# Last attention group, its projection and the last rows by halves of the queries, in a two-layer gated cross-attention and MoE kernel

## The reference, cut to what matters

```python
x = x + tanh(g_xattn[1]) * xattn(layernorm(x), ctx)     # 16 heads of 16
#   out = softmax(q k^T * scale) v
#   h = relu(out @ W1 + b1);  return h @ W2 + b2         # 256 -> 512 -> 256
x = x + tanh(g_ffn[1]) * moe(layernorm(x))
#   logits = xn @ Wg + bg                                # 8 experts, top 2
#   h = relu(xn @ W1[e] + b1[e]); eo = h @ W2[e] + b2[e]; mixed by softmax of the top 2; layernorm
# layernorm(x) = (x - mean) / sqrt(var + 1e-5)
```

## Time and profile before

| | |
|---|---|
| median of 3 runs | 1501.73 us (1501.42 to 1502.45) |
| profiled execution, its own time | 1500.18 us |
| span of its records | 1498.4 us |
| TensorE busy, mean granted clock | 1351.1 us (90%), 0.951 |
| TensorE weight loads busy | 716.5 us (48%) |
| ScalarE busy | 975.1 us (65%) |
| VectorE busy | 549.3 us (37%) |

### The profile page before, as it was taken

How to read it: one execution, slowest core, us unless ns; L and a number is a source line. 1 busy time by engine, 2 the same in 40 slices (tenths; PEclk the granted TensorE clock), 3 DMA queues, 4 the chain that set the end, 5 groups by cost and what they waited for, 6 DMA issues and landing times. The chain is left out here.

```text
span 1498.4 us, 31951 instructions
## 1 busy us (share of the span) xinstructions
PE 1351.1 (90%) x13236; PEld 716.5 (48%) x13236; DVE 549.3 (37%) x1242; ACT 975.1 (65%) x1162; POOL 175.6 (12%) x188
## 2 busy tenths in 40 slices
PE   7799999999999996999657999999999994399994
PEld 4433333333333654999533334334334333299983
DVE  7412152242423253443550222422422524544435
ACT  4499999999996323333137996995996990055532
POOL 2000000000001321333200000000000000166530
PEclk9899999999999997999878999999999997599997
DMA  7661010101011714111439110110111115012214
GB/s 209 157 119 27 20 26 20 27 20 26 23 33 60 247 56 142 40 47 47 109 93 179 26 27 15 34 27 16 33 27 46 65 33 166 18 58 75 72 59 166
DMA packets 65866, 100.82 MB, mean 67 GB/s; under 512 B 10074, under 2 KB 47966, under 8 KB 64952
## 3 DMA queue, kind: packets, MB, share of 16 engines
q1 hardware_dynamic: 59768, 82.47, 20.2%
q0 software_dynamic: 5952, 16.26, 3.3%
HBM read 67.99 MB, written 26.21 MB: 63 GB/s over the span
## 5 line engine op out<-in xcount | busy, mean ns | idle before, releaser
L1182 ACT ACTIVATE arena<-ps 128x1024 f32<-128x1024 f32 x556 | 553.9, 1219 | 57.2 <-PE ps L948 57.2
L948 PE MATMUL ps<-arena 99*32 99x512 bf16 x6656 | 465.9, 384 | 15.4 <-PEq L798 9.4
L948 PEld LDWEIGHTS ps<-arena 99*32 99x32 bf16 x6656 | 151.3, 95 | 405.8 <-issue 167.0
L1182 ACT ACTIVATE wqkv<-ps 128x1024 f32<-128x1024 f32 x276 | 294.3, 1221 | 22.7 <-PE ps L948 22.7
L964 PE MATMUL ps<-arena 128*32 128x512 f32 x2224 | 290.5, 594 | 1.0 <-ACT arena L1182 0.8
L1264 DVE COPY work<-ps 128x512 f32<-128x512 f32 x32 | 22.1, 692 | 405.4 <-PE ps L964 405.4
L1652 PEld LDWEIGHTS ps<-work,arena 128*128 128x128 f32 x1184 | 144.6, 195 | 6.5 <-DVE work L1745 3.5
L1652 PE MATMUL ps<-work,arena 128*128 128x128 f32 x1184 | 145.7, 279 | 2.1 <-DVE work L1745 2.1
L964 PE MATMUL ps<-wqkv,arena 128*32 128x512 f32 x1104 | 144.0, 593 | 0.0
L1842 POOL DMA_INDIRECT work<-xn_img,fetch x62 | 60.9, 983 | 628.7 <-POOLq L928 612.8
L1664 PE MATMUL ps<-arena,work 128*128 x496 | 117.2, 380 | 0.0
(11 more groups left out here) (204 smaller groups left out, 1157.7 us busy)
## 6 DMA issues: line engine op xcount, KB each, us to landing
arena<-in_ew SPq DMA_DIRECT2D x16, 512.0 KB, 5.3
arena<-q_img SPq DMA_DIRECT2D x32, 192.0 KB
arena<-y_tok SPq DMA_DIRECT2D x12, 512.0 KB, 6.3
arena<-k_img SPq DMA_DIRECT2D x8, 624.0 KB, 12.9
q_img<-work SPq DMA_DIRECT2D x18, 256.0 KB, 2.6
k_img<-work SPq DMA_DIRECT2D x21, 208.0 KB, 2.5
arena<-q_img SPq DMA_DIRECT2D x32, 128.0 KB
work<-work SPq DMA_DIRECT2D x128, 32.0 KB, 2.0
```

The costliest lines, as they stand in the source:

```text
L948: last = nc.tensor.matmul(ps[i * VW:(i + 1) * VW, buf + j, :], k2[0:ROWS + SHIFT, h, at:at + VW], q2[0:ROWS + SHIFT, h, :], start=True, st ...
L1182: nc.scalar.activation(probs[(b * STEPS + u) % RING], ps[:, buf:buf + 2, :], ACT.Exp, scale=SCALE).then_inc(s_exp, 1)
```

## The change

It has four parts.

1. The last group (both layers). VectorE's new `last_group` drops the copy of the bank, spreads the sums as before, and then inverts and multiplies the first 256 queries and after them the second 256, reading the bank itself. SyncE's new `gather_last` moves each half with 4 DMAs of its own (8 in all, each of half the size) as soon as it is multiplied; the second half has a semaphore of its own, `s_oh2`. In layer 0, TensorE's first pair of projection tiles waits also until both halves are multiplied, the second pair for the second half's DMAs.
2. Layer 1's `last_projection` makes all hidden blocks of the first half (16 matmuls of 256 columns instead of 8 of 512), then of the second, then the output of the first two tiles, then of the last two. VectorE's new `own_tail` follows in halves.
3. The bias b2 of the last rows is added to x ahead of time (gate times b2), so x is updated straight from the banks. Each pair of tiles takes its statistics at once.
4. The router's rows: xn gets only the mean taken off before the rows are turned; Newton's steps and the scaling of xn by the inverse root come after that, once the rows are turned (`s_rt`), and the logits are scaled by the inverse root as the router's bias is added (4 instructions of 8 columns instead of 1 of 32). SyncE stores the last rows after the scaling.

```diff
+        def norm_means(n):
             for t in range(n):
                 last = nc.vector.bn_aggr(mv[:, t, :], stats[:, t, :])
+            return last
+        def norm_root(step, n):
+            step(norm_means(n))
+            norm_newton(step, n)
...
                         t = 2 * pair + half
+                        if b == NB - 1 and half == 0:
+                            pe.wait_ge(s_on, NB * NG + 1)
+                        if b == NB - 1 and t == 2:
+                            pe.wait_ge(s_oh2, 16 * HG)
...
                     def last_projection():
-                        for i in range(2):
-                            pe.wait_ge(s_oc[i], NB * 16 * HG * NG // 2)
-                        pe.wait_ge(s_u, NB * NG)
-                        for f in range(4):
-                            for k in range(KD):
-                                last = nc.tensor.matmul(ps[:, f, :], w1[:, k, f * P:(f + 1) * P], oT[:, k, :],
-                                                        start=(k == 0), stop=(k == KD - 1))
+                        for half in range(2):
+                            cols = slice(half * 2 * P, (half + 1) * 2 * P)
+                            if half:
+                                pe.wait_ge(s_oh2, 16 * HG)
+                            else:
+                                for i in range(2):
+                                    pe.wait_ge(s_oc[i], NB * 16 * HG * NG // 2)
+                                pe.wait_ge(s_on, NB * NG)
+                            for f in range(4):
+                                if half:
+                                    pe.wait_ge(s_read7, use(NB, f))
+                                for k in range(KD):
+                                    last = nc.tensor.matmul(ps[:, f, cols], w1[:, k, f * P:(f + 1) * P], oT[:, k, cols],
+                                                            start=(k == 0), stop=(k == KD - 1), skip_group_check=True)
+                                last.then_inc(s_full7, 1)
+                        for half in range(2):
+                            if half:
+                                pe.wait_ge(s_on, NB * NG + 1)
+                            for f in range(4):
+                                pe.wait_ge(s_read7, use(NB, 4 * half + f))
+                                for t in range(2 * half, 2 * half + 2):
+                                    last = nc.tensor.matmul(ps[:, 4 + t, 0:D],
+                                                            hidT[:, f, t * P:(t + 1) * P], w2[:, f, :],
+                                                            start=(f == 0), stop=(f == 3))
                             last.then_inc(s_full7, 1)
...
+                    def last_group():
+                        g, n = NG - 1, NB * NG
+                        dve.wait_ge(s_pv, NB * NG * NC)
+                        nc.vector.stream_shuffle(out=sums, in_=ps[:, 6 + g % 2, :], mask=[DH] * VW).then_inc(s_copy, 1)
+                        dve.wait_ge(s_copy, n)
+                        for i in range(2):
+                            cols = slice(i * 2 * P, (i + 1) * 2 * P)
+                            nc.vector.reciprocal(sums[:, cols], sums[:, cols]).then_inc(s_inv, 1)
+                            if i == 0:
+                                dve.wait_ge(s_oc[g % 2], (NB * NG // 2 - 1) * 16 * HG)
+                            dve.wait_ge(s_inv, n + i)
+                            nc.vector.tensor_tensor(o_norm[:, g % 2, cols], ps[:, 6 + g % 2, cols], sums[:, cols],
+                                                    ALU.mult).then_inc(s_on, 1)
+                        dve.drain()
...
+                    def own_tail():
+                        last_group()
+                        for half in range(2):
+                            cols = slice(half * 2 * P, (half + 1) * 2 * P)
+                            for f in range(4):
+                                dve.wait_ge(s_full7, use(NB, 4 * half + f))
+                                nc.vector.tensor_scalar(hidT[:, f, cols], ps[:, f, cols], b1[:, f:f + 1], 0.0,
+                                                        ALU.add, ALU.max).then_inc(s_read7, 1)
+                        for pair in range(2):
+                            dve.wait_ge(s_full7, use(NB, 8 + pair))
+                            rows = x[:, (NB - 1) * TB + 2 * pair:(NB - 1) * TB + 2 * pair + 2, :]
+                            nc.vector.scalar_tensor_tensor(out=rows, in0=ps[:, 4 + 2 * pair:6 + 2 * pair, 0:D], scalar=tg,
+                                                           in1=rows, op0=ALU.mult, op1=ALU.add).then_inc(s_xup[pair], 1)
+                            dve.wait_ge(s_xup[pair], NB)
+                            for i in range(2 * pair, 2 * pair + 2):
+                                nc.vector.bn_stats(stats[:, i, :], x[:, (NB - 1) * TB + i, :])
+                        dve.drain()
+                        step(norm_means(TB))
+                        for i in range(TB):
+                            last = nc.vector.tensor_scalar(xn[:, (NB - 1) * TB + i, :], x[:, (NB - 1) * TB + i, :],
+                                                           mv[:, i, 0:1], None, ALU.subtract)
+                        last.then_inc(s_ends, 1)
+                        norm_newton(step, TB)
+                        dve.wait_ge(s_rt, 1)
+                        for i in range(TB):
+                            last = nc.vector.tensor_scalar(xn[:, (NB - 1) * TB + i, :], xn[:, (NB - 1) * TB + i, :],
+                                                           rstd[:, i:i + 1], None, ALU.mult)
+                        last.then_inc(s_xs, 1)
...
+                        elif b == NB - 1:
+                            for t in range(TB):
+                                last = nc.vector.scalar_tensor_tensor(out=lg[:, b * TB + t, :], in0=got_logits[:, t, :],
+                                                                      scalar=rstd[:, t:t + 1], in1=rb[:, :],
+                                                                      op0=ALU.mult, op1=ALU.add)
...
-                    tail(NB, NB - 1)
+                    if l == 1:
+                        for pair in range(2):
+                            rows = x[:, (NB - 1) * TB + 2 * pair:(NB - 1) * TB + 2 * pair + 2, :]
+                            nc.vector.scalar_tensor_tensor(out=rows, in0=b2[:, :, :], scalar=tg, in1=rows, op0=ALU.mult,
+                                                           op1=ALU.add)
+                        dve.drain()
+                        own_tail()
+                    else:
+                        tail(NB, NB - 1)
                     route(NB - 1)
...
+                    def gather_last():
+                        g = NG - 1
+                        for i in range(2):
+                            cols = slice(i * 2 * P, (i + 1) * 2 * P)
+                            sp.wait_ge(s_on, NB * NG + i)
+                            for j in range(HG):
+                                h = HG * g + j
+                                sp.dma_start(oT[(h % 8) * DH:(h % 8 + 1) * DH, h // 8, cols],
+                                             o_norm[j * VW:j * VW + DH, g % 2, cols]
+                                             ).then_inc(s_oh2 if i else s_oc[g % 2], 16)
...
-                        sp.wait_ge(s_ends, NB)
+                        sp.wait_ge(s_xs, 1)
                         store_rows(NB - 1)
```

More of the change, by code:

```diff
@@ L433, in consts_pool, with norm_newton @@
                            allow_small_or_imprecise_dtypes=True)
-        def norm_root(step, n):
+        def norm_means(n):
             for t in range(n):
                 last = nc.vector.bn_aggr(mv[:, t, :], stats[:, t, :])
-            step(last)
+            return last
+        def norm_root(step, n):
+            step(norm_means(n))
+            norm_newton(step, n)
+        def norm_newton(step, n):
             step(nc.vector.tensor_scalar(var_e[:, 0:n], mv[:, 0:n, 1], EPS, None, ALU.add))
@@ L889, in layer @@
             s_xup = [sem(f"x_updated{l}_{i}") for i in range(2)]
+            s_oh2 = sem(f"oT_last_half_in{l}")
             s_ln = sem(f"moe_params_in{l}")
@@ L1277, in tail @@
                     def tail(b, now, first_group=None):
-                        group(now, NG - 1)
+                        if b == NB:
+                            last_group()
+                        else:
+                            group(now, NG - 1)
                         k = 0
-                        own = L.mlp and b == NB
                         if L.mlp:
@@ L1284, in tail @@
                                 dve.wait_ge(s_full7, use(b, k))
-                                nc.vector.tensor_scalar(hidT[:, f, :], ps[:, f if own else 7, :], b1[:, f:f + 1], 0.0,
+                                nc.vector.tensor_scalar(hidT[:, f, :], ps[:, 7, :], b1[:, f:f + 1], 0.0,
                                                         ALU.add, ALU.max).then_inc(s_read7, 1)
@@ L1290, in tail @@
```

(3 more changed lines are left out.)

## The result

| | before | changed |
|---|---|---|
| median, first comparison (6 runs each) | 1502.09 us (1501.33 to 1506.28) | 1491.20 us (1489.51 to 1495.98) |
| profiled execution, its own time | 1500.18 us | 1492.88 us |
| span | 1498.4 us | 1491.1 us |
| mean granted clock | 0.951 | 0.955 |

A forecast was written before the change was run, and what follows sets the result against it. From the attention's end in layer 1 to the logits, one engine works at a time. Savings of 7.4 + 0.45 - 0.45 + 0.25 = 7.65 us from 1501.73 gave 1494.1 us, range 1491.6 to 1497.0.

The forecast's parts named there:

- first half at TensorE: Layer 1's last group: copy dropped and first half sent early, so TensorE starts the projection at 1242.87, 2.49 us earlier.
- projection to output: Layer 1's hidden layer, from its start to the output's start: 7.07 us of matmuls plus 2.0 lost to low clock.
- output's end to turning: Layer 1's update and means: 3.5 us instead of 8.55, with the first pair covered and Newton's steps moved behind.
- turning to logits' step: Router's turning, copies and logits: 6.71 us before, less half of 0.93 for turning, with logits at the low clock.
- the logits' step: VectorE's scaling of the logits, 4 instructions of 8 columns instead of one: 0.45 us more.
- layer 0: Layer 0's projection: copy gone and halves there earlier, gaining between 0 and 0.89 us, taken as 0.25.
- The median of the runs is 1.55 above it: Base of the forecast: the median lies 1.55 us above the profiled 1500.18, so the sum is taken from 1501.73.
- about 1 us either way by the clock: Spread given to the forecast itself, from when TensorE's clock rises; each microsecond later costs 0.5.
- the clock high through the logits: Rival: TensorE's clock stays high through turning and logits until VectorE's scaling binds; 9.6 us gain, 1492.1 us; chance 0.14.
- The first half coming no earlier: Rival: TensorE in effect waits for all 8 DMAs, starting about 1245.3; 5.2 us gain, 1496.5 us; chance 0.15.
- the slower case: Rival: the clock does not rise in layer 1's projection; 5.0 us slower, 1506.7 us; chance 0.03.
- nothing: Rival: something else releases the experts' block, so the time stays at 1501 us; chance 0.04.

The follow-up runs named there:

- e11: Kernel before with extra unused matmuls in all TensorE waits from the attention's end to the experts' first tile in layer 1: 1494.06 us, ratio 0.9955.
- e12: Changed kernel with extra unused matmuls in all TensorE waits from layer 1's attention to the experts' first tile, same program as e8: 1487.17 us, ratio 0.9908.
- e3: Changed kernel with the halves undone in layer 1 only, 512 columns at once; other parts stay: 1495.34 us, ratio 0.9966.
- e5: Kernel before with extra unused matmuls in TensorE's waits: 10 ahead of the projection, 8 ahead of turning, 1 ahead of the logits: 1498.13 us, ratio 0.9982.
- e7: Changed kernel with each half's 4 DMAs in layer 1 issued by SyncE and ScalarE, two each: 1493.02 us, ratio 0.9946.
- e2: Changed kernel with part 4 alone undone, so xn is normalized whole before the rows are turned: 1496.72 us, ratio 0.9976.
- e8: Changed kernel with extra unused matmuls in all TensorE waits from the attention's end to the experts' first tile in layer 1: 1487.29 us, ratio 0.9917.
- e10: The changed kernel measured again without any edit: 1489.37 us, ratio 0.9922.
- e4: Changed kernel with extra unused matmuls in TensorE's waits: 7 ahead of the projection, 3 ahead of turning, 1 ahead of the logits: 1488.41 us, ratio 0.9922.
- e9: Changed kernel with extra unused matmuls in all those TensorE waits (as e8, but 6 ahead of the projection) and two DMA queues as in e7: 1486.67 us, ratio 0.9909.

## Why the prediction was wrong

**Each step against its measure** (changed kernel's first profile):

| term | predicted | measured |
|---|---|---|
| first half at TensorE | 2.49 earlier | 2.68 by the start, 0.07 of it from before the group: 2.61 |
| projection to output | 9.07 | 8.79 (clock's rise after 3.7, not 4.0) |
| output's end to turning | 3.5 | 3.31 (the subtractions took 1.14, not 1.38) |
| turning to logits' step | 6.30 | 5.88 (turning wholly at the high clock) |
| the logits' step | +0.45 | +0.44 |
| layer 0 | 0.25 | 0.25 at its place (10.40 us instead of 10.65 from the shared expert's start to the projection, load idle 0.24 instead of 0.89), 0.07 left at the last group |

The path came out 8.45 us shorter against my 7.65 less 0.25, 7.4. Mechanism, order and places held: no gap between the halves, the root hidden, VectorE free before the logits were. The rule of the Trainium skill (VectorE: DVE Perf Modes, Rules for kernel authors) against a larger count of VectorE operations, cited in the prediction, cost nothing here: the two inversions take 1.75 and 1.74 us where the one took 3.35, and what that is more lies behind what TensorE waits for. No run undoes the dropped copy, the early b2 or layer 0's part alone; what they are worth is read from rows.

**The step that failed** is "The median of the runs is 1.55 above it", and with it "about 1 us either way by the clock". I took a difference between one execution and the median of three for a constant, and forecast from 1501.73. Over five sets of runs the kernel before has a median of 1500.2 with single executions from 1496.8 to 1506.3; the changed kernel's profiled execution was 1.7 above its median, not 1.55 below it. These 3.2 us cover the whole miss of 2.9, for the profiled execution itself came as forecast (span 1490.8 forecast, 1491.1 measured). That was luck in part: its path was 1.05 us shorter than my sum, and its rest, in which I had put no difference, 1.2 us longer. Nor is the base the only thing off. In the first comparison the kernel before stood at 1502.09, and the gain was 10.9 instead of 7.65. Over all runs the forecast is 3.6 us above the changed kernel's 1490.5: 1.5 by the base and 2.1 by the gain. From 1500.2 the sum of 7.65 gives 1492.6, still 1.4 above the 1491.20 measured.

**What the sum did not hold.** The gain is 9.7 us over all runs, and the path gives 6.8 to 8.45. With extra matmuls in all waits the medians' difference is 6.9, near the path's 6.7 (e11, e12). So some 2.8 us of the gain are not there where the clock is mostly held; from the runs' spread I estimate an error of 1.5 us on this. It points to TensorE's clock, outside my terms, but it is not shown: the extra work occupies TensorE too, and no plain changed kernel stands beside that pair. That the levels of one kernel go with the clock is on record: of the changed kernel's 17 runs the ten with a mean granted clock of 0.956 or 0.957 took 1488.1 to 1490.9 us, the two with 0.952 took 1494.5 and 1496.0. What was seen of it in the profiles: turning at the high clock in one of three profiles (0.9), the rise in the projection between 3.7 and 5.2 us after its start (0.8), the rise at the start of the experts' loop after 7 or after 13.5 us, and the clock's fall ahead of the last sums. With these the rest moves between 194.0 and 200.8 in kernels that do not differ there.

The two places in the rest can be told apart. Where the rise at the loop's start comes late (e3, e5, e7), the sixth fetch is 17.8 to 18.0 us behind the first, and 14.8 to 16.1 in the others. From the last fetch to the end 55.6 to 56.6 us pass where the clock does not fall ahead of the last sums (e2, e3, e8, e10, e11), 57.9 to 59.3 where it does, and 60.1 to 60.2 in e5 and e7, where it stays low longer. A third spread lies ahead of the path: the last group begins between 1233.8 and 1237.7, and layer 0's 0.25 us cannot be seen in that. Whether the shorter waits of the change make the good cases more frequent there, or whether chance fell so in three sessions, stays open; 14 profiles do not settle it.

My rivals: the clock high through the logits was not seen in the changed kernel, and e4 shows its price: 58.00 - 54.58 = 3.4 us, of which 1.8 are the projection's (8.79 less 6.98) and the other 1.6 are near the 1.95 that I gave it. The first half coming no earlier is refuted by the start at 1242.68 and by e3, the slower case by the rise at 1246.36, "nothing" by the fetch.

## What to carry to other kernels

A chain with one engine at work at a time is added up well from single rows, and halving pays where the first half's way is the only one waited for. Before a sum is set against a median, ask how wide single executions lie; where they differ by 6 us and more, three runs don't give a base to 1 us, and the range must have that width whatever the sum's own error. Where a matmul engine's clock falls in each wait, work whose result nobody reads can hold it; here that was worth 2.4 us in the changed kernel (e4) and 1.4 in the kernel before (e5). It also takes the clock out of most of the comparison of two kernels, though not all of their spread: e8's runs still lie 7.7 us apart.

## What the hardware showed that I had not expected

The clock falls also while TensorE has work. In e12 there was no idle time over 0.75 us from the extra matmuls on, and still it fell at 1265.44, behind turning, one extra matmul and the logits (the first and last of eight such rows), and under the extra matmuls ahead of the counts. In e8, the same program, it did not fall there; in e9 it did.

```profile
1260.41 1.09 PE L1019 MATMUL ps<-ident,xn 128*128 128x128 f32 x8 [0.73 <-DVE xn L1346]
1261.34 1.02 PE L1126 MATMUL ps<-w,ones 128*128 128x512 f32 x2
1262.67 0.39 PE L1026 MATMUL ps<-rw,arena 128*128 128x8 f32 x2 [0.31 <-ACT work L1220]
...
1264.26 0.37 PE L1026 MATMUL ps<-rw,work 128*128 128x8 f32 x2
...
1264.48 4.52 PE L1126 MATMUL ps<-w,ones 128*128 128x512 f32 x6
```

```profile
1265.00:1266.00 1.00, 1.00 (x3) 0.72 0.80 324
```

The logits' 16 instructions of 8 columns take 1.96 us at the high clock (1262.67 to 1264.63), 0.12 each, more than half of what one of 256 columns takes in the output (7.07 / 32 = 0.22). So it is not the columns alone that set it; I take it for the loading of weights, which no run here tested. Eight DMAs of half the rows' length take 4.93 us to issue where four of the whole took 2.40: the issue has the price of a DMA, not of its bytes.
